# Attention's running maxima spread differently over the qkv slots and the attention units, and the score banks paired from unit 9

## The reference, cut to what matters

```
q, k, v = qkv[:, :, 0], qkv[:, :, 1], qkv[:, :, 2]
attn = jnp.einsum('nthd,ntkd->nthk', q * scale, k)
attn = jax.nn.softmax(attn, axis=-1)
out = jnp.einsum('nthk,ntkd->nthd', attn, v)
```

## Time and profile before

| what | us |
|---|---|
| median of 3 runs | 400.33 (400.14 to 400.94) |
| the profiled execution, its own time | 400.57 |
| its span, first to last instruction | 398.4 |
| TensorE busy | 373.5 (94%) |
| VectorE busy | 262.6 (66%) |
| ScalarE busy | 207.0 (52%) |
| GpSimd busy | 133.1 (33%) |
| mean granted TensorE clock | 0.99 |

### The profile page before, as it was taken

How to read it: one execution, slowest core, us unless ns; L and a number is a source line. 1 busy time by engine, 2 the same in 40 slices (tenths; PEclk the granted TensorE clock), 3 DMA queues, 4 the chain that set the end, 5 groups by cost and what they waited for, 6 DMA issues and landing times.

```text
span 398.4 us, 10250 instructions
## 1 busy us (share of the span) xinstructions
PE 373.5 (94%) x4035; PEld 243.4 (61%) x4035; DVE 262.6 (66%) x771; ACT 207.0 (52%) x436; POOL 133.1 (33%) x152
## 2 busy tenths in 40 slices
PE   8999999999988999999986888799999999999996
PEld 4665545556544777677654555577656666656675
DVE  2688885677688866664475354568897958475552
ACT  4356454443134788988884576656675243231200
POOL 6029999989543900002120000036300101001130
PEclk9999999999999999999998899999999999999999
DMA  5999200000000134441145120000000000000011
GB/s 167 289 336 267 90 2 3 2 18 2 2 0 16 30 50 72 63 61 33 41 47 51 14 29 2 2 2 2 2 1 2 30 16 17 29 17 29 16 46 45
DMA packets 44021, 19.34 MB, mean 49 GB/s; under 512 B 36605, under 2 KB 42337, under 8 KB 43848
## 3 DMA queue, kind: packets, MB, share of 16 engines
q1 hardware_dynamic: 43974, 18.69, 20.2%
HBM read 13.89 MB, written 4.73 MB: 47 GB/s over the span
## 4 chain that ended last, share of the span: by engine, by line
PE 72%; DVE 16%; ACT 7%; issue 4%; DVEq 0%; ACTq 0%
PE psum L1030 14%; PE psum L1046 13%; PE psum L600 7%; PE psum L901 6%; PE psum L955 4%; PE psum L706 2%; PE psum L860 2%; PE psum L969 2%; ACT stage L1170 2%; PE psum L1007 2%; DVE MX L1444 2%; PE psum L941 2%; PE psum L718 2%; DVE scratch L1414 2%; PE psum L662 2%
## 5 line engine op out<-in xcount | busy, mean ns | idle before, releaser
L1030 PE MATMUL psum<-scratch,W 128*128 128x512 f16 (+1 forms) x252 | 57.9, 379 | 0.0
L1046 PE MATMUL psum<-W,big 128*128 128x288 f16 x432 | 55.1, 286 | 0.0
L1266 ACT ACTIVATE big<-psum 128x512 f32<-128x512 f32 x36 | 21.3, 597 | 57.3 <-PE psum L1030 52.5
L901 PE MATMUL psum<-WQ,scratch 128*128 128x288 f16 (+1 forms) x336 | 49.1, 286 | 1.6 <-DVE scratch L1435 1.2
L1046 PEld LDWEIGHTS psum<-W,big 128*128 128x128 f16 x432 | 42.2, 98 | 12.9
L594 POOL TENSOR_TENSOR X<-X,scratch 128x288 f32<-128x288 f32 x16 | 13.5, 856 | 83.6 <-DVE big L1595 83.6
L1214 ACT ACTIVATE big<-psum 128x1024 f32<-128x1024 f32 x32 | 32.3, 1024 | 17.2 <-PE psum L941 17.2
L1030 PEld LDWEIGHTS psum<-scratch,W 128*128 128x128 f16 (+1 forms) x252 | 24.6, 98 | 25.6
L901 PEld LDWEIGHTS psum<-WQ,scratch 128*128 128x128 f16 (+1 forms) x336 | 31.0, 98 | 10.2 <-issue 2.5
L589 POOL TENSOR_TENSOR X<-X,big 128x288 f32<-128x288 f32 x16 | 13.0, 826 | 70.2 <-ACT big L1241 69.9
L600 PE MATMUL psum<-ident 128*32 128x192 f32 (+3 forms) x124 | 35.7, 372 | 0.0
(11 more groups left out here) (230 smaller groups left out, 770.7 us busy)
## 6 DMA issues: line engine op xcount, KB each, us to landing
X<-in_x_dram SPq DMA_DIRECT2D x4, 576.0 KB, 15.4
value_rows<-scratch SPq DMA_DIRECT2D x16, 144.0 KB, 2.4
out_dram<-big SPq DMA_DIRECT2D x16, 144.0 KB, 1.7
big<-in_L_cond_W_dram SPq DMA_DIRECT2D x1, 2268.0 KB
big<-in_L_cond_ada_w_dram SPq DMA_DIRECT2D x2, 864.0 KB, 18.0
big<-value_rows SPq DMA_DIRECT2D x48, 36.0 KB, 2.5
stage<-in_L_cond_fc_w_dram SPq DMA_DIRECT2D x1, 1296.0 KB, 18.1
big<-in_L_cond_fc_w_dram SPq DMA_DIRECT2D x1, 1152.0 KB
```

Source lines behind the costliest of these rows:

```text
L901: mm = pe.matmul(UB[gu % 2][:, 0:D], HT[0:r, n % 2, a_, P * a:P * a + P], WQ[0:r, w_, D * w:D * w + D], start=(p_ == 0), stop=(p_ == 6))
L1030: mm = pe.matmul(FB[idx % 3], W1[0:r, w_, P * m:P * m + P], HT[0:r, n % 2, a_, :], start=(p_ == 0), stop=(p_ == 6))
L1046: mm = pe.matmul(YB[t % 2][:, 0:D], g[:, a_, f, cols], W2[:, w_, f, :], start=(f == 0 and a_ + w_ == 0), stop=(f == NF - 1 and w_ == 1))
L1266: act.activation(G32[:, idx % 2, :], FB[idx % 3], ACT.Gelu, scale=1.0 / (FINE * FINE)).then_inc(gelu_sb, 1)
```

## The change

Step s of the maxima moves to slot 21 + 9s//8 for s from 0 to 23: slots 21 to 28, 30 to 37, 39 to 46, so v slots have one too, but for 29 and 38. The other eight stand one each in stages 0 to 7. PAIRED goes from 12 to 8, ROWS_AFTER from 11 to 7, and all copies of the sums go to VectorE (DVE_AT from 9 to 4, and ScalarE's function for it is gone).

```diff
-        AHEAD = {24 + 3 * s_ // 2: s_ for s_ in range(16)}
-        LATER = {st: 1 if st < 4 else 2 for st in range(10)}
-        ROWS_AFTER = 11
-        PAIRED = 12
-        DVE_AT = 9
+        AHEAD = {21 + 9 * s_ // 8: s_ for s_ in range(24)}
+        PAIRED = UNITS - len(AHEAD)
+        ROWS_AFTER = PAIRED - 1
+        DVE_AT = 4
@@ later(st)
-            return [16 + sum(LATER.get(i, 0) for i in range(st)) + k for k in range(LATER.get(st, 0))]
+            return range(len(AHEAD) + st, min(len(AHEAD) + st + 1, UNITS))
@@ ScalarE
-            def values_out(w):
-                act.wait_ge(pv_ready, 4 * w + 4)
-                if w >= 1:
-                    act.wait_ge(o_turned, 2 * w)
-                for c_ in range(2):
-                    act.copy(by_row(OT[c_]), by_tile(PO[c_])).then_inc(ot_ready, 1)
-
...
-                if st < DVE_AT:
-                    if st >= 4 and st % 4 == 0:
-                        values_out(st // 4 - 1)
```

## The result

| | before | after |
|---|---|---|
| ratio of times, 95% interval | | 0.9937 (0.9918 to 0.9956) |
| lowest run, us | 400.06 | 397.53 |
| median over all 20 runs, us | 402.14 | 398.42 |
| profiled execution, own time, us | 400.57 | 401.14 |
| mean granted TensorE clock in it | 0.990 | 1.000 |

The account below looks back on a forecast made before the run. TensorE bounds qkv, with little idle time; unpaired attention with two maxima a stage has it busy only 7.72 of 11.80 us. Attention -6.9 plus qkv +5.2 gives -1.7: 398.9 from the profile, 398.6 from the median, 398.7 taken; range 396.4 to 401.0.

Parts of the forecast that it names:

- Slots 21 to 28: In qkv: four added steps delay slot 28's product by 2.9 us, with a 1.5 us wait at slot 27.
- The v slots: In qkv slots 32, 35, 41 and 44: each added step costs 0.57 us, 2.3 for four.
- The end of qkv: The end of slot 48, set by the last cast, doesn't move: 0 us.
- Attention: From scores(4) to scores(13): 14.97 us instead of 21.89, a gain of 6.9, with scores(9) at 9.1.
- The copies' move to VectorE at nothing: In attention: moving two copies from ScalarE to VectorE counted at nothing beyond the half stage already stepped.
- The clock: In old attention: TensorE at 1.2 instead of 2.4 GHz from about 216.3 to 223.7, counted inside the 6.9 us gain.
- (b): In attention: the clock still falls once, after stages 4 to 7, costing 1.6 us; time 400.3, no change; chance 0.12.
- (a): In qkv: added steps cost 0.34 us each without waits, 2.7 in all; time 396.1; chance 0.12.
- (c): In qkv around slot 27: the clock falls, losing 2.5 to 3.7 us; time about 401.7; chance 0.10.
- (d): In attention: SP's row 2 comes late and unit 16 waits; 399.7 to 401.7 at 1 to 3 us beyond; chance 0.05.
- Attention's start: Sign of a wrong prediction: attention starting later than 202.7 or earlier than 201, against 197.52 before.

Follow-up runs that it names:

- split last: The changed kernel, but in slots with a maximum and a turned block VectorE takes the split after the maximum: qkv 46.04 us against 46.91, ratio 0.9923.
- filled kernel: The kernel before, with three dummy matmuls between the two maxima of stages 4, 5, 6, 8 and 9: attention 19.75 us, ratio 0.9956.
- run with twenty steps: The changed kernel with twenty maxima in qkv instead of 24, two in each of attention stages 4 to 7: qkv 44.28, attention 20.87, 404.87 us, no ratio.
- last run: The changed kernel, VectorE taking maxima first in qkv and maximum(31) ahead of the first normalisation in attention: attention 14.29 us, ratio 0.9820.
- maxima-first run: The changed kernel, but in every slot with a maximum VectorE takes it first, then low, then the split: qkv 42.74 us, ratio 0.9816.

## Why the prediction was right, step by step

398.7 was predicted; the median shown with the kernel before, times the ratio, is 400.33 x 0.9937 = 397.8. The gain was 2.5 instead of 1.7, and each term of the sum was near its measure.

- **Slots 21 to 28**, +2.9 forecast, +2.63 measured. By slot, from product to product, it is 0.35, 0.52, 0.51, 0, 0.16, 0.36 and 0.73. The place and the cause of the largest wait, the maximum behind the split behind the table load, were right: 1.41 against 1.5. Undoing the order on VectorE (split last) takes 1.09 of it away.
- **The v slots**, 0.57 each forecast, 0.55 measured (2.21 for four, and 30.97 - 28.75 with those four alone): 0.57 in three of them and 0.50 in slot 32. The cause was right too, VectorE's maximum standing behind low; what the prediction did not see is that it is only an order in a list. With the maxima first, all these waits are gone.
- **The end of qkv** was counted at nothing and came 0.17 earlier, as the table of row 1 no longer waits for the last maximum. Stage 0 lost 0.18 again, since its maxima wait for ScalarE's copy of that table, 0.52 instead of 0.29. Together nothing, and that was luck: neither was in the sum.
- **Attention**, -6.9 forecast, -7.21 measured. scores(9) was at 8.82 after scores(4), not 9.1. Half of the difference was there by scores(7), the copies of stage 4 ending some 0.1 earlier than stepped; the other half came in stage 7, where scores(8) begins 0.39 after maximum(31) ends, not 0.5.
- **The copies' move to VectorE at nothing**: wrong as a statement. On ScalarE they cost 0.67 more. The sum was right since I had stepped the stages with the copies where the change puts them.
- **The clock**: the term that I never took out. "In that are the lower clock of the old stretch and ten stages' waits" stands in the sum as one number. The filled kernel divides it: 2.1 us are the clock, 5.1 are the rest, which is the doubled stages and, within it, 0.67 for the copies' move if that is worth the same in the old kernel, which no run shows. So against a kernel whose clock doesn't fall the change gains 5.1 and costs 4.85 (4.67 in qkv, 0.18 in stage 0), nearly nothing, and nearly all of the net gain of 2.36 is the clock. The doubled stages are six, 4 to 9, not the ten that the prediction speaks of; ten stages have a step, and the change leaves four of them as they are. The low stretch is also a little shorter than the prediction's 7.4 us: a mean of 0.54 over 7.5 us is 6.9 us at half. For rival (b) I had put the price of a fall under paired units at 1.6; the run with twenty steps shows 2.3.
- **Pairing from unit 9**: the prediction counted stages, not this part by itself, and so was not misled, but my theory after the result was. It brings nothing here: what pairs save goes into the stage with the earlier transposition. The wait for maximum(31) is a part of that, as the last run shows.

Of the rivals, (a) did not come about, but what it would have needed, steps without waits, is what the maxima-first run makes. (b) and (c) had the clock fall; it stayed at 1.00 in all of the changed kernel's qkv from slot 21 on and in its attention, and fell in the kernel with twenty steps and double stages, after 62% busy. (d), SP's row, did not come near: scores(16) was 7.2 us earlier after scores(4) than before, not the 10 or so of the prediction. One of its signs of being wrong was badly set. Attention's start was to be no later than 202.7, which is 197.52 + 5.2, the forecast itself; in the profile it is at 205.46, because slot 21 is late. By distances it is 46.91 - 42.24 = 4.67 later than before, 202.19 on the old axis and within the bounds.

Not tried: fillers in the twenty-step kernel, the copies on VectorE in the old one, and pairing from unit 13 with normalise moved.

## What to carry to other kernels

A step that an engine takes from another engine's hand should stand in its list by when its input comes, not by the order in which the code speaks of it: here 4.2 us lay in reductions queued behind operations that waited for a third engine. Before work is moved to give an engine its time back, ask what part of the loss is a lower clock after many short waits; a few dummy matmuls in the waits measure it, and here they gave nearly the whole gain. A saving that needs an earlier transfer or transposition has to pay for the wait that this one meets in its new place.

## What was not expected of the hardware

TensorE's clock fell to its lower level, 1.2 GHz, for some 7 us in the old kernel and in the one with twenty steps, though its longest wait before was 1.18 us in the old one; it had been busy 65% and 62% of the 11 to 12 us ahead. It did not fall in the changed kernel, 83% busy over 8.8 us, nor in the filled one, 88% over 13.1, though single waits there were as long: 1.41 us in the changed kernel's slot 27, 1.18 in the filled one. In the 30 executions of the kernel before that entered the ratios of the experiments the mean granted clock was 0.986 to 0.991, but for one of 0.996; in all of the changed kernel's that entered its own it was 0.999 or 1.000. The fall belongs to the program, not to a single run.
